# Two halves of a projection two slots apart, and a logarithm placed last in its slot

## The reference

```
xz = x @ Win.T;  u, z = split(xz)                 # 256 channels each: two halves of 128
u  = silu(causal_conv(u))
dtr, B, C = split(u @ Wx.T)
dt = softplus(dtr @ Wdt.T + bdt)                  # relu(a) + log(1 + exp(-|a|))
h  = exp(dt * A) * h + (dt * u) * B               # over 512 positions, 16 states
y  = (h . C + u * D) * silu(z)
```

## Time and profile before

| | |
|---|---|
| median of 3 timed runs | 2490.19 us (2486.5 to 2494.22) |
| the profiled execution's own time | 2493.17 us |
| its span, first to last instruction | 2491.4 us |
| DVE busy | 2303.9 us, 92% of the span |
| PE busy | 2069.2 us, 83% |
| POOL busy | 1926.9 us, 77% |
| ACT busy | 1504.6 us, 60% |
| mean granted TensorE clock | 0.929 of full |

### The profile page before, as it was taken

One profiled execution on the slowest core, in us unless ns is written; L12 is line 12 of the kernel. 1 busy time (PEld: TensorE's weight loads), 2 busy tenths in 40 slices (PEclk: granted clock), 3 DMA queues, 4 the chain that ended last, 5 costly groups with the idle time before them and its releaser, 6 DMA issues. The chain is left out here.

```text
span 2491.4 us, 31612 instructions
## 1 busy us (share of the span) xinstructions
PE 2069.2 (83%) x9893; PEld 1310.2 (53%) x9893; DVE 2303.9 (92%) x3850; ACT 1504.6 (60%) x2467; POOL 1926.9 (77%) x1254
## 2 busy tenths in 40 slices
PE   6677988888798887979878797887989888798868
PEld 2345655555465554645555565554545555465554
DVE  4999999999999999999999999999999999999963
ACT  4556666566656656655566666656665666666523
POOL 2777878888787888878788787888878788787844
PEclk7789989989999999999999999998989999899979
DMA  5333342333434233333433334342333433333310
GB/s 153 134 132 121 119 133 103 132 119 106 132 112 141 102 132 120 109 131 111 134 106 120 125 112 134 114 136 104 120 128 108 135 110 118 127 111 126 111 47 5
DMA packets 112284, 291.17 MB, mean 117 GB/s; under 512 B 18292, under 2 KB 44900, under 8 KB 112116
## 3 DMA queue, kind: packets, MB, share of 16 engines
q1 hardware_dynamic: 112116, 289.15, 34.4%
HBM read 282.77 MB, written 6.34 MB: 116 GB/s over the span
## 5 line engine op out<-in xcount | busy, mean ns | idle before, releaser
L451 POOL TENSOR_TENSOR bt<-v,bb 128x1024 f32<-128x1024 f32 x511 | 1205.9, 2360 | 188.3 <-DVE psA L872 173.7
L872 DVE TENSOR_TENSOR_SCAN psA<-psA,bt 128x512 f32<-128x512 f32 x1024 | 1195.5, 1213 | 61.3 <-ACT psA L628 60.6
L628 ACT ACTIVATE psA<-dt,aneg 128x512 f32<-128x512 f32 x1024 | 688.0, 688 | 731.9 <-DVE g L882 731.5
L1125 PEld LDWEIGHTS psY<-ident,g 128*128 128x128 f32 x4096 | 503.3, 149 | 432.2 <-DVE g L882 214.8
L1125 PE MATMUL psY<-ident,g 128*128 128x128 f32 x4096 | 599.3, 289 | 135.7 <-DVE g L882 134.3
L882 DVE TENSOR_TENSOR g<-psA,cb 128x512 f32<-128x512 f32 x1024 | 671.5, 675 | 0.0
L541 POOL TENSOR_TENSOR act<-pf,gf 128x512 f32<-128x512 f32 x288 | 366.1, 1271 | 288.4 <-DVE pf L971 256.7
L1215 PE MATMUL F<-h2T,w 128*128 128x512 f32 x576 | 327.6, 652 | 94.5 <-DVE pf L971 93.5
L1254 PE MATMUL F<-w,act 128*128 128x128 f32 x2304 | 315.0, 281 | 15.4 <-DVE facc L985 8.3
L1218 PE MATMUL F<-h2T,w 128*128 128x512 f32 x576 | 313.5, 628 | 0.0
L1254 PEld LDWEIGHTS F<-w,act 128*128 128x128 f32 x2304 | 287.6, 196 | 31.3 <-POOL act L541 27.3
(11 more groups left out here) (178 smaller groups left out, 1760.3 us busy)
## 6 DMA issues: line engine op xcount, KB each, us to landing
bb<-bc_rows SPq DMA_DIRECT2D x256, 512.0 KB, 3.8
cb<-bc_rows SPq DMA_DIRECT2D x256, 512.0 KB, 3.7
x<-in_L_attn_x SPq DMA_DIRECT2D x16, 256.0 KB, 4.3
out_x<-osb SPq DMA_DIRECT2D x16, 256.0 KB, 4.6
modA<-mod_table SPq DMA_DIRECT2D x15, 192.0 KB, 4.5
w<-in_L_ffn_ew SPq DMA_DIRECT2D x2, 1024.0 KB, 7.3
bc_rows<-xd SPq DMA_DIRECT2D x32, 64.0 KB, 3.2
modG<-mod_table SPq DMA_DIRECT2D x16, 64.0 KB, 4.1
```

What stands on the lines that cost most here:

```text
L451: g.tensor_tensor(bt[:, n % 2, :, :], v[d][:, :, :], bb[:, n // 2 % 2, n % 2, :].unsqueeze(1).broadcast_to([P, NH, T]), ALU.mult).then_inc ...
L628: s.activation(psA[:, half * T:half * T + T], dt_[d][:, half, :], ACT.Exp, scale=aneg[d][:, half, n:n + 1]).then_inc(a_s, 1)
L872: w.tensor_tensor_scan(ah, ah, bt[:, n % 2, half, :][:, order], 0.0, ALU.mult, ALU.add)\
L1125: last = m.matmul(psY[:, half * T + i * P:half * T + i * P + P], g_[:, n % 2, half, i * P:i * P + P], ident[:, :], is_transpose=True, star ...
```

## The change

The first half of z is projected a slot earlier (slots 9 and 28 in place of 10 and 29) and the second half stays where it was (slots 11 and 30), on PE, ACT and DVE alike (the three places with `k - Z_AT` in the diff are ACT, DVE and PE in this order). And ACT's `ln1p`, in slots 9 and 28, now comes after the experts' side work and the prep of its slot, in place of before them.

```diff
-U_AT, XD_AT, DT_AT, LN1P_AT, Z_AT, V_AT = 0, 6, 7, 9, 10, 11
+U_AT, XD_AT, DT_AT, LN1P_AT, Z_AT, V_AT = 0, 6, 7, 9, 9, 11
 ...
-                if k - Z_AT in (0, 1):
-                    silu(b, d, Z, k - Z_AT)
+                if k - Z_AT in (0, 2):
+                    silu(b, d, Z, (k - Z_AT) // 2)
 ...
-                    if scan and not last and slot == PREP_SLOT[0] + LN1P_AT:
-                        ln1p(b + 1, 0)
-                    if scan and slot == PREP_SLOT[1] + LN1P_AT:
-                        ln1p(b, 1)
                     if scan:
 ...
                     if scan:
                         side(b, slot, True, None if last else b + 1)
+                    if scan and not last and slot == PREP_SLOT[0] + LN1P_AT:
+                        ln1p(b + 1, 0)
+                    if scan and slot == PREP_SLOT[1] + LN1P_AT:
+                        ln1p(b, 1)
 ...
-                if k - Z_AT in (1, 2):
-                    silu(b, d, Z, k - Z_AT - 1)
+                if k - Z_AT in (1, 3):
+                    silu(b, d, Z, (k - Z_AT) // 2)
 ...
-                if k - Z_AT in (0, 1):
-                    open_piece(Z, k - Z_AT)
-                    m.matmul(psP[:, :], wzT[d][:, k - Z_AT, :], xnT[:, PAD:PAD + T], start=True, stop=True)\
+                if k - Z_AT in (0, 2):
+                    half = (k - Z_AT) // 2
+                    open_piece(Z, half)
+                    m.matmul(psP[:, :], wzT[d][:, half, :], xnT[:, PAD:PAD + T], start=True, stop=True)\
                         .then_inc(pP_full, 1)
```

## The result

The changed kernel takes 2473.8 us (median of 5 runs, 2470.9 to 2475.8) against 2486.5 us (5 runs, 2485.7 to 2494.2) of the kernel before, measured together: a ratio of 0.994, 95% interval 0.9924 to 0.9957. It is faster by more than the 0.3% that can be told from nothing.

The account below looks back on a forecast made before the run. DVE (92% busy) was held by slot 12's stall, the logarithm and POOL's chain. Batches 1 to 14: 20.0 - 1.8 - 8.4 = 9.8 us won; batch 15 wins 1.1, batch 0 loses 0.6: 10.3, forecast 2482 us, range 2474 to 2490.

Parts of the forecast that it names:

- The stall of slot 12: Slot 12, batches 1 to 15: DVE's wait for the expert's tanh, 21.4 us in total, would go.
- The first `zs` hidden in the waits: DVE's `zs` (0.68 us), moved to slots 10 and 29, would hide in scan waits of 1.69 and 0.74 us.
- The product in time for the first tanh: Slots 9 and 28: the z product would end before the tanh needs it, 2 and 0.4 us to spare.
- rival 3: Slot 28: PE at half clock makes the first tanh 2.7 us late; 2501 us, slower than before; chance 0.09.
- POOL caps the freed batches: From `dt` to step 16, POOL becomes the limit in batches freed of the stall; each gives 0.16 us back.
- rival 1: POOL doesn't cap slots 9 to 16, so DVE's own path counts: 16.3 us won, 2477 us; chance 0.10.
- So the logarithm, `dt`, and the decays behind it are 0.6 later: Slots 9 and 28: a tanh before the table load delays these 0.6 us, costing 8.4 us over 14 batches.
- The base: Starting time for the gain: profiled 2493.2 us gives 2482.9, the 3.0 lower median 2479.9; 2482 was taken.
- Rival 2, the phase of the clock: Slot 12: timed runs have more batches without a stall, so 5.8 us of gain are missing; about 2486; chance 0.17.
- Rival 4, nothing happens: Slots 11 and 12: ACT's queue slips 1.3 us, so the stall stays in another form; 2490 to 2493; chance 0.09.

Follow-up runs that it names:

- e3: Kernel before with one edit on PE: in slot 11 the experts' up products are issued ahead of the second half of z; 2468.3 us, ratio 0.9922.
- e6: Kernel after with one of POOL's two passes over the norm in slot 12 left out (modulation's shift not added); 2468.4 us, ratio 0.9913.
- e7: Kernel before with slot 11's up products ahead of the second half of z, and one POOL pass of slot 12 left out; 2472.1 us, ratio 0.993.
- e1: Kernel after with the logarithm put back right behind the decays, so only z is split; 2468.6 us, ratio 0.9927 to before.
- e5: Kernel after with a second tanh, into an unread tile, ahead of the first silu half in slots 9 and 28; 2490.8 us, ratio 0.9997.
- e8: Kernel before, unaltered, run again for its profile; 2493.4 us.
- e9: Kernel before, unaltered, run once more for its profile; 2484.2 us.
- e2: Kernel before with only the logarithm's lines moved behind the side work, giving the same instruction order on every engine; 2489.7 us, ratio 1.0004.
- e4: Kernel after, unchanged, measured again; 2472.5 us, ratio 0.9945.

## Why the prediction was right, and where it was wrong

**The stall of slot 12 goes: right.** 21.4 us in the profiled execution, all of it, in all batches. That it would go "even at half clock" is not shown, as slot 11 was at 1.00 in every batch. e3 shows the mechanism as it was put: the up products queued behind a z product that waited. ACT's queue was said to be 0.6 us ahead of `pf`; it is 0.85.

**The first `zs` hidden in the waits: right in slot 10, where it stands ahead of a wait of 1.61 us.** In the bare slot the decays' wait of 0.23 reappears, as forecast.

**The product in time for the first tanh: right.** Among all waits of ACT, over the whole span of the kernel before:

```profile
ACT th L649 <- PE psP L1157: 42.5, 31, 2.0
```

In the kernel after ACT's waits have no row for this tanh at all, in slots 9 and 28 or elsewhere. In slot 28 of batches 1 to 14 the product takes 1.02 to 1.03 us and ends 0.45 us or more ahead of the tanh, where 0.4 had been forecast. So rival 3, the slower case, didn't occur: the granted clock was 1.00 there in all of these batches, in three profiles.

**POOL caps the freed batches: right.** The new waits for `bt` and e6 show it, and refute rival 1. With the logarithm early POOL's cap is small: e3 takes 38.27 us from scan 10 to 18 and e7 38.14, close to the 0.16 that the prediction let a freed batch give back. e1 takes 38.36, as much as e6 with POOL relieved (38.38), and has no wait for `bt`: there DVE's own path decides.

**"So the logarithm, `dt`, and the decays behind it are 0.6 later": the mis-sized term.** It is 0.52. From the start of the second decay to the table load there were 0.71 us before (1110.54 to 1111.25 in batch 7); in batch 7 of the kernel after there are 1106.23 - 1105.01 = 1.22, with the tanh between, and another count by e5 gives 0.49. The 0.6 is the length of a tanh; what an added one costs is the distance from start to start, as the next begins before the last has ended. That is 0.1 us too much in each batch: 38.8 us from scan 10 to 18 where 38.9 stood. In slots 28 to 31 the forecast set 0.6 of the tanh against 0.6 of `zs` and said zero; it is a gain of 0.08 each, the same 0.1 again. In 14 batches the two are worth 1.5 and 1.2 us; with 0.4 for batch 0 (0.2 lost, not 0.6) they make, within 0.1 us, the middle part's 13.3 us out of the forecast's 10.3.

**The base: the step that failed.** The prediction set the sum against the profiled execution's 2493.2 us and against the median, and settled near the former, because "a run that is 3 us quicker may be one in which one or two batches more fell on the pattern without stall". The profiles of e8, e9 and e2 show otherwise. The first profiled execution had the smallest loss of the four, 21.4 us, and e9, which is 9 us quicker as a whole, has 21.9: this quick run had no less to give. The first one was slow for a reason in its last part, 6.55 us at a lower clock, which has nothing to do with the stall.

Of the 8.2 us between the forecast and the measured time, 5.2 are this base and 3.0 the gain. The forecast stands on 2482.0 + 10.3 = 2492.3, while 2473.8 + 13.3 is 2487.1, and the kernel before, timed beside the change, had a median of 2486.5. By the parts of the profile, 2493.2 - 6.55 - 13.3 = 2473.3. That it meets the measured 2473.8 so closely is in part luck, as the 2.4 us ahead of the first scan are left in it. Had the gain been the forecast's 10.3, this sum would give 2476.3, inside the range; had the base been 2492.3, a gain of 13.3 would give 2479.0, inside it too. It took both to leave the range.

**Rival 2, the phase of the clock: right in kind, wrong in sign.** The loss does vary from execution to execution, 21.4 to 25.9 us. The Trainium skill, TensorE: Matmul & The Clock Gate, Part 1: The HAM clock gate, has the chip judge activity in windows that aren't aligned to the kernel, and these four sums of one order of instructions agree with it. But the profiled execution lay at the low end of the spread, and the rival had assumed that it lay at the high one. I had treated the spread of the timed runs as a spread of stalls alone; in the four profiles of before's order the stall differs by 4.5 us, the last part by 6.5 (100.7 to 107.2) and the stretch ahead of the first scan by 3.6 (45.2 to 48.8).

**Rival 4, nothing happens: refuted.** `pf` has one wait of 0.2 us left in all. The logarithm's move does nothing by itself, as it changes no engine's order (e2); together with z split it costs 4 to 6 us (e1 against the kernel after).

**Two orders that beat the change.** e3, the kernel before with the up products of one slot ahead of the z product, takes 2468.3 us (ratio 0.9922), and e1 2468.6. Both beat the change by about 4 us (e4, 2472.5, beside them): z split or up first, the logarithm stays where it was. Both at once was not run.

## What to carry to other kernels

When an engine waits at a buffer, ask what is queued behind the wait and who wants that: moving the wanted work ahead of the waiting instruction won as much here (e3, 2468.3 us) as removing the wait (e1, 2468.6). An instruction put ahead of the head of a chain that has no slack is paid for every time, at its start-to-start distance. And before a profiled execution becomes the base of a forecast, cut it into parts and look for one in which the clock, not the kernel, was slow.

## What the runs showed of the chip

**ACT's instructions overlap at their ends.** ACTIVATEs of 128x512 last 0.58 to 0.60 us each but start 0.47 to 0.48 apart (1114.90, 1115.38, 1115.85 in the timeline of after), and an added one costs 0.48 to 0.50 us per place in e5.

**The last part took one of three lengths.** 100.7, 102.8 or 107.2 to 107.4 us in 13 profiles of kernels that do the same in it, with DVE, ACT and POOL equally busy; the granted clocks are 0.90, 0.87 and 0.82. Before's order alone was seen at two of them; what selects among the three wasn't found.

**The price of a stall depended on when TensorE's clock was at its lower level,** 1.2 instead of 2.4 GHz: nothing to 2.31 us a batch for identical instructions. In the kernel after the clock dips in slot 12 (0.64 to 0.97) when the wanted products are done, and that costs nothing.
